# Reordering the second layer of a graph network: attention before the ball mixer, queries kept on chip, two weight jobs in other stages

## The reference, cut to what matters

```
xn = layernorm(x)
x = x + gnn0(xn, W, edges) + mix0(xn)          # message sum; low-rank attention and feed-forward
x = x + ffn0(layernorm(x))                     # 8 experts, all of them
xn = layernorm(x)
x = x + gnn1(xn, src, dst) + mix1(xn)          # the two terms do not depend on each other
x = x + ffn1(layernorm(x))                     # shared expert, and the best 2 of 8 experts

def gnn1(feat, src, dst):
    q, k, v = feat @ Wq.T + bq, feat @ Wk.T + bk, feat @ Wv.T + bv
    score = clip(sum(q[dst] * k[src], per head) / sqrt(32), -10, 10)
    alpha = softmax of score over the edges of one destination
    wv = segment_sum(alpha * v[src], dst)
    x = feat + wv @ Wp.T + bp
    return x + gelu(layernorm(x) @ W1.T + b1) @ W2.T + b2

def mix1(x):                                   # "ball mixer": projections to a ball, a convolution
    ...                                        # (its middle tap only), batch norm, linear attention
```

## Time and profile before

| | us |
|---|---|
| median of 3 runs | 3988.4 |
| lowest, highest | 3985.86, 3989.91 |
| the profiled execution | 3987.43 |
| its span in the profile | 3985.7 |
| granted TensorE clock, mean | 0.807 |

### The profile page before, as it was taken

How to read it: one execution, slowest core, us unless ns; L and a number is a source line. 1 busy time by engine, 2 the same in 40 slices (tenths; PEclk the granted TensorE clock), 3 DMA queues, 4 the chain that set the end, 5 groups by cost and what they waited for, 6 DMA issues and landing times. The chain is left out here.

```text
span 3985.7 us, 66521 instructions
## 1 busy us (share of the span) xinstructions
PE 2587.3 (65%) x17122; PEld 2086.2 (52%) x17123; DVE 2170.5 (54%) x4408; ACT 1269.1 (32%) x2467; POOL 1315.5 (33%) x1017
## 2 busy tenths in 40 slices
PE   4413333436678699996375434777777487699997
PEld 4413333323367477774254423555555366589986
DVE  6523333322456388885237764777777555544445
ACT  0300010003143255553257732222222243345441
POOL 0048888853000000000001024888888500211115
PEclk9855555557679599997597767999999778699998
DMA  1046666730000000001200015777777200356643
GB/s 36 32 105 157 156 165 162 197 94 6 0 22 0 16 11 13 16 16 46 73 0 0 0 40 150 193 189 187 189 191 189 52 21 0 124 188 229 227 159 91
DMA packets 255391, 373.00 MB, mean 94 GB/s; under 512 B 119009, under 2 KB 180889, under 8 KB 250965
## 3 DMA queue, kind: packets, MB, share of 16 engines
q0 software_dynamic: 154752, 174.53, 18.2%
q1 hardware_dynamic: 87700, 185.50, 14.2%
q10 hardware_dynamic: 12864, 12.06, 1.1%
HBM read 320.09 MB, written 50.96 MB: 93 GB/s over the span
## 5 line engine op out<-in xcount | busy, mean ns | idle before, releaser
L750 POOL DMA_INDIRECT ms_got<-gather,ms_index x400 | 506.2, 1265 | 124.9 <-issue 114.4
L1689 POOL DMA_INDIRECT as_gkv<-gather_kv,as_index x340 | 462.0, 1359 | 108.7 <-issue 100.9
L811 PE MATMUL ms_total<-ms_got,ms_hot 125*125 125x256 f16 x1040 | 231.0, 410 | 376.8 <-DMA ms_got<-gather,ms_index 251.9
L811 PEld LDWEIGHTS ms_total<-ms_got,ms_hot 125*125 x1040 | 202.9, 219 | 405.0 <-issue 405.0
L2097 POOL MEMSET bm_fx<- 128x128 f32 x1 | 0.2, 205 | 1013.0 <-POOLq L115 1013.0
L1810 PE MATMUL as_total<-as_gkv,as_hot 125*125 125x264 f32 x850 | 218.8, 406 | 78.0 <-DVE as_summed L555 65.6
L1478 ACT ACTIVATE ex_h<-ex_up,ex_now 128x313 f32<-128x313 f32 (+1 forms) x320 | 196.1, 613 | 197.2 <-PE ex_up L458 190.0
L1810 PEld LDWEIGHTS as_total<-as_gkv,as_hot 125*125 125x125 f32 x850 | 157.7, 193 | 117.8 <-issue 91.8
L2791 DVE CAST moe_hidden<-moe_h 128x256 f16<-128x256 f32 (+1 forms) x336 | 101.8, 303 | 209.9 <-ACT moe_h L2728 209.3
L2728 ACT ACTIVATE moe_h<-moe_up,moe_w 128x256 f32<-128x256 f32 (+1 forms) x336 | 163.1, 487 | 135.2 <-PE moe_up L458 93.2
L1784 PE MATMUL as_picked<-y_rows,as_pick 125*125 x1060 | 150.3, 291 | 52.6 <-issue 47.7
(11 more groups left out here) (448 smaller groups left out, 5895.2 us busy)
## 6 DMA issues: line engine op xcount, KB each, us to landing
moe_w<-wsplit SPq DMA_DIRECT2D x34, 2052.0 KB
as_dsts<-in_dst SPq DMA_DIRECT2D x83, 305.2 KB
wsplit<-ms_split SPq DMA_DIRECT2D x36, 512.0 KB
ms_raw<-in_L_ffn_W1p SPq DMA_DIRECT2D x16, 512.0 KB
ms_raw<-in_L_ffn_W2p SPq DMA_DIRECT2D x16, 512.0 KB
results<-moe_made SPq DMA_DIRECT2D x32, 256.0 KB, 8.2
ms_got<-gather,ms_index POOLq DMA_INDIRECT x400
gather_kv<-qkv_out SPq DMA_DIRECT2D x5, 1250.0 KB
```

The lines of the kernel that those rows point to most:

```text
L750: pool.indirect_dma_start(out=got[:, s, j, :], out_offset=None, in_=m.gather0, in_offset=bass.IndirectOffsetOnAxis(ap=index[:, s, j:j + 1] ...
L811: ins = pe.matmul(total[:, visit % RING, 0:C], hot[:, visit % RING, j, :], got[:, s, j, p * C:(p + 1) * C], start=(j + p == 0), stop=(j + ...
L1689: pool.indirect_dma_start(out=gkv[s][:, j, 0:2 * C], out_offset=None, in_=m.gather_kv, in_offset=bass.IndirectOffsetOnAxis(ap=index[:, s, ...
```

## The change

- The order of the stages: `attention_sum`, `attention_out`, a layernorm and `feed_forward` "ff1" come right behind `query_rows`; `ball_log_rows` and `ball_mixer` come after them, before the last layernorm. `m.y` is taken once and given back before the ball mixer.
- The f16 halves of the queries are written straight into `m.y` (`m.q16`); they are neither stored nor loaded back, and TensorE no longer waits for them in `attention_sum`.
- The turner runs in `edge_tables`: after each of the 20 counting steps TensorE turns one or two blocks, ScalarE copies and stores them before it takes the square root of the degrees.
- The splitter runs in `feed_forward` "ff1" (`splits=True`): 4 steps in each of the first 4 chunks and 2 in the last.
- In `attention_out` the bias bp is a third product per tile (a row of ones with the bias) and no longer an addition on GpSimd.
- `feed_forward` loses its form for several experts, which was not used.

```diff
-def edge_tables(nc, m, src, dst):
+def edge_tables(nc, m, a, src, dst):
...
             @block.scalar
             def _(act):
+                for i in range(2):
+                    turner.load(act, i)
+                turner.store(act)
                 act.wait_ge(s_span, 2)
                 act.activation(m.degree_s[:, 0, :], m.degree_s[:, 0, :], ACT.Sqrt).then_inc(s_rows, 1)
+                turner.finish(act)
...
+                steps, blocks = ET // SET, len(turner.blocks)
+                for i in range(steps):
+                    pe.wait_ge(s_hot, i + 1)
+                    add(i % 2, i == 0, i == steps - 1)
+                    turner.turn(pe, range(blocks * i // steps, blocks * (i + 1) // steps))
...
 def message_sum(nc, m, a):
-        turner = Turner(nc, m, a, ph)
-        splitter = Splitter(nc, m, a, ph)
...
-                        if splits and s % 2:
-                            splitter.low(dve, i, s // 2)
...
-                    turner.turn(pe, part, PARTS)
...
+def feed_forward(nc, m, a, name, W1, b1, W2, gain, bias_in, splits=False):
+    PIECES = 4
...
             def _(sp):
+                sp.dma_start(w1_32, W1.rearrange("(b p) n -> p b n", p=128)).then_inc(s_w, 16)
+                sp.dma_start(w[:, CB * F:].rearrange("p (b n) -> p b n", b=FB),
+                             W2.rearrange("(b p) n -> p b n", p=128)).then_inc(s_w, 16)
+                if splits:
+                    with sp.Fori(0, X8) as e:
+                        for h in range(2):
+                            splitter.move(sp, e, h)
+                    for h in range(2):
+                        splitter.move(sp, X8, h)
+                    splitter.finish(sp)
...
+                def highs(c, own, k):
+                    if splits and (own or k < 2):
+                        for s in range(2):
+                            splitter.high(act, c * PIECES + k, s)
+
+                def chunk(c, own):
+                    for u in range(units):
+                        f, (at, n) = u // 2, HALVES[u % 2]
+                        act.wait_ge(s_up, c * units + (u + 1))
+
+                        act.wait_ge(s_hidden, c * units + max(u - 3, 0) + AHEAD)
+                        act.activation(h32[:, u % 4, 0:n], up[:, u % 4, 0:n], ACT.Gelu,
+                                       scale=1.0 / WS, bias=bias[:, f:f + 1]).then_inc(s_h32, 1)
+                        if u % 8 == 3:
+                            highs(c, own, u // 8)
+                    highs(c, own, 2)
+                    highs(c, own, 3)
...
+                def lows(c, own, k):
+                    if splits and (own or k < 2):
+                        for s in range(2):
+                            splitter.low(dve, c * PIECES + k, s)
...
+                        if u % 8 == 7:
+                            lows(c, own, u // 8)
+                    for j in range(J):
...
+                        if j in (2, 4):
+                            lows(c, own, 1 + j // 2)
...
 def query_rows(nc, m, a):
-                    sp.dma_start(m.gather_q.rearrange("(t p) n -> p t n", p=R)[:, bass.ds(c * J, J), :],
-                                 q16[:, s, :, :, :].rearrange("p j k n -> p j (k n)")).then_inc(s_stored[s], 16)
...
-                        act.activation(q16[:, s, j, 0, :], out[:, s, j, 0:C], ACT.Copy).then_inc(s_high, 1)
+                        act.activation(m.q16[:, c * J + j, 0, :], out[:, s, j, 0:C], ACT.Copy).then_inc(s_high, 1)
...
 def attention_sum(nc, m, dst):
-                sp.dma_start(q16.rearrange("p t k c -> p t (k c)"),
-                             m.gather_q.rearrange("(t p) n -> p t n", p=R)).then_inc(s_q, 16)
...
-                pe.wait_ge(s_q, 16)
...
 def attention_out(nc, m):
-                    for rows_, bias in ((m.z, bp), (m.x, b2)):
-                        some = rows_[:, bass.ds(c * J, J), :]
-                        ins = pool.tensor_tensor(some, some, repeat_mid(bias, J), ALU.add)
-                    ins.then_inc(s_bias, 1)
+                    some = m.x[:, bass.ds(c * J, J), :]
+                    pool.tensor_tensor(some, some, repeat_mid(b2, J), ALU.add).then_inc(s_bias, 1)
...
-                            ins = pe.matmul(bank[:, j % 4, 0:C], cols[:, j, b, :], w[:, b, :],
-                                            start=(b == 0), stop=(b == CB - 1))
+                            pe.matmul(bank[:, j % 4, 0:C], cols[:, j, b, :], w[:, b, :],
+                                      start=(b == 0), stop=False)
+                        ins = pe.matmul(bank[:, j % 4, 0:C], m.ones[0:1, 0:R], bp[0:1, :], start=False, stop=True)
...
         query_rows(nc, m, a)
-        ball_log_rows(nc, m)
-        free_y()
-        ball_mixer(nc, m, a)
-        take_y(1)
         attention_sum(nc, m, a["dst"])
         attention_out(nc, m)
         layernorm(nc, m, "ln5", m.y)
-        feed_forward(nc, m, "ff1", 1, lambda e: m.turned["w1"], col["L1_gnn_b1"], lambda e: m.turned["w2"],
-                     gain=col["L1_gnn_ln_g"], bias_in=col["L1_gnn_ln_b"])
-        free_y()
+        feed_forward(nc, m, a, "ff1", m.turned["w1"], col["L1_gnn_b1"], m.turned["w2"],
+                     col["L1_gnn_ln_g"], col["L1_gnn_ln_b"], splits=True)
+        y_stack.close()
+        ball_log_rows(nc, m)
+        ball_mixer(nc, m, a)
```

More of the change, by code:

```diff
@@ L178, in edge_tables @@
         s_hot, s_count, s_v = ph.sem("hot"), ph.sem("count"), ph.sem("v")
+        turner = Turner(nc, m, a, ph)
         with nc.Block() as block:
@@ L565, in finish @@
         self.dve.sem_inc(s_pace, 1)
[L568 to L608, removed]
-            name, W, o, k, taps = self.blocks[i]
-            kb = k // 128
-            act.wait_ge(self.s_turned, i + 1)
-            if i + 2 < n:
-                self.load(act, i + 2)
-            if i >= 2:
-                act.wait_ge(self.s_out[i % 2], 16 * (i // 2))
-            act.activation(self.cols[:, i % 2, 0:kb, :], self.bank[:, i % 2, 0:kb, :], ACT.Copy)\
-                .then_inc(self.s_cols, 1)
-            act.wait_ge(self.s_cols, i + 1)
-            act.dma_start(self.m.turned[name].rearrange("(b p) n -> p b n", p=128)[:, :, o * 128:(o + 1) * 128],
-                          self.cols[:, i % 2, 0:kb, :]).then_inc(self.s_out[i % 2], 16)
-    def finish(self, act):
-        n = len(self.blocks)
-        act.wait_ge(self.s_out[0], 16 * ((n + 1) // 2))
-        act.wait_ge(self.s_out[1], 16 * (n // 2))
@@ L906, in feed_forward, with part, every_chunk @@
             ph.sem(x) for x in ("up", "h32", "hhigh", "hidden", "down", "added"))
-        ph.ahead(s_h32, s_hidden, s_down, s_added)
+        splitter = Splitter(nc, m, a, ph) if splits else None
+        if splits:
+            splitter.s_pace = s_pace
+        ph.ahead(s_hidden, s_down, s_added, s_h32)
         units = FB * len(HALVES)
         w1_32 = w[:, 0:CB * F].rearrange("p (b n) -> p b n", b=CB)
-        def part(s, k, layer, b, at, n):
+        def part(k, layer, b, at, n):
             start = b * F + at if layer == 0 else CB * F + b * C + at
-            return w16[:, s, k, start:start + n]
+            return w16[:, k, start:start + n]
+        def every_chunk(eng, work):
+            with eng.Fori(0, CHUNKS - 1) as c:
+                work(c, True)
+            work(CHUNKS - 1, False)
         with nc.Block() as block:
@@ L1059, in mixer0 @@
+                every_chunk(dve, chunk)
 def mixer0(nc, m, a):
```

339 lines of the change are left out of this document (135 added, 204 removed).

## The result

The changed kernel takes 4036.9 us (median of 4 runs, 4032.1 to 4045.7) against 3987.1 us (4 runs), a ratio of 1.0128 with a 95% interval of 1.0108 to 1.0149: slower by 1.3%, 6 us under the forecast of 4043 and inside the range. The profiled execution took 4034.7 us, span 4033.0, so it lies 47.3 us over the span before.

What follows compares the result with a forecast made beforehand. GpSimd bounds the message and attention sums, TensorE the second feed-forward, in a chain of stages with barriers. Terms -24 + 15 - 22 - 39 + 7 + 119 = +56 gave 4043 us; 8-in-10 range 3998 to 4090.

Steps and rivals of the forecast that it cites:

- Feed-forward, +119: Second feed-forward: with the split moved in, waits for its loads lengthen the stage by 119 us (ends +55 and +168).
- 17L + 108: Second feed-forward: time from chunk 0's first subtraction to the end, 249 us against 133 before, excluding 3 us for lower clock.
- L: Splitter in the second feed-forward: time from a step's second subtraction until both next halves are loaded, taken as 8.3 us.
- Attention output, +7: Attention output: bias products cost TensorE 2.2 us more a chunk, stage 7 us longer (0 to +10).
- Edge tables, +15: Edge tables: the turner's 26 blocks fit only in part beside the counting steps and delay the square root, +15 us.
- Message sum, -24: Message sum: less stretched gathers save 9 us and the turner's missing tail 14.7 us, together -24 (-19 to -29).
- Queries -22: Queries, keys and values: without the queries' stores, computing becomes the bound, -22 us (-18 to -25).
- attention sum -39: Attention sum: TensorE's first pick no longer waits for queries, so GpSimd never waits for its index, -39 us (-35 to -42).
- (a): Second feed-forward: loads run at nearly full rate, L = 5.2, +3 us, whole kernel 3990 us; chance 0.12.
- (b): Second feed-forward: the split hides almost wholly behind TensorE, L = 4, -17 us, whole kernel 3970 us; chance 0.10.
- (c): Second feed-forward: transfers as slow as in the message sum, L = 10.9, +100 us, whole kernel 4087 us; chance 0.17.
- (d): Attention sum: first pick waits for destinations slowed by gathers, the stage keeps its 39 us, whole kernel 4082 us; chance 0.06.

Runs made afterwards that it cites:

- the nine kernels: Nine kernels, the changed one included, that neither split nor turn weights in the message sum; that stage took 627.6 to 636.0 us, mean 631.5.

## Why the prediction came out right, and its missed term

By its own steps:

- **Feed-forward, +119 against +104.** The mechanism holds, in form and in place. From the first up product to the end it took 2979.7 - 2741.4 = 238.3 us, and 17L + 108 with the measured L of 7.66 is 238.2. That it agrees to 0.1 us is luck: the four rounds of a chunk took 197.4 us where 4 x (4L + 20) is 202.6, and the rest made up for it; with the blocks loaded once the form gives 173.4 us where 179.5 were measured. Off were L, taken as 8.3 (17 x 0.64 = 11 us), a choice between two rows and no measurement, and the 3 us added for the lower clock, which the form didn't need although TensorE was granted only 0.77. (In the kernel before, the first chunk's 96 up products took 15.67 us at a granted 0.82, those of each later chunk 12.97 at 1.00.) The forecast's sign "under 210 us: then L is below 5.5" doesn't fit its own form either, by which 210 us is an L of about 4.8.
- **Attention output, +7 against +25: the failed step.** "Five more cost 2.2 us a chunk" priced a product over one partition by a row of products over 128. Over 65 or 125 partitions that price holds: 46.0 and 47.1 us are +7 and +8. The single partition adds 55.6 - 47.1 = 8.5 us (25 x 0.38 = 9.5 by the rows), and in this execution the clock, which rose 25 us into the stage instead of 6 to 8, another 64.1 - 55.6 = 8.5. The bound of +10 was too low as well: the nearest row had another shape.
- **Edge tables, +15 against +10.4.** The square root is 10.3 us later (118.86, before 108.52). The 4 us of waits that were added for the small blocks did not come: up to the two blocks of eight transposes a counting step begins every 3.26 us. The large ones made TensorE wait for 5.1 us together. One part had no term: ScalarE loads a table for the square root, which it did at 4.24 us before, while it had nothing to do; now it does so behind the last copy, and the square root waits for these 1.28 us.

```profile
117.56 1.28 ACT L315 ACT_TABLE_LOAD   x1 [0.43 <-ACT edg_cols L203]
118.86 0.23 ACT L315 ACTIVATE degree_s<-degree_s 125x25 f32<-125x25 f32 x1
```

- **Message sum, -24 against -27.0**, and against -23.1 for the mean of the nine kernels. The parts were shown apart: the kernel with only the split put back has longer gathers and no tail, the one with only the turner put back has the tail. The tail is 14.6 to 15.0 us each time (15.9 to 16.2 against 1.2 to 1.3); the 9 us for the gathers is a mean over kernels that differ by as much.
- **Queries -22 against -23, attention sum -39 against -38.6.** Both came back when the queries' way through memory did. The 3.5 us of landing and barrier and the 2 us of landing were estimates: before, the next stage began 1.5 us after the last traffic (none from 1940.2 on), and after the change 12.5 us after the last store's issue at 1888.1, where the forecast had 13.6.
- **Rivals.** (a) and (b) needed L of 5.2 and 4. The fixed part of a load behind the 5.2 was an estimate; no run shows one apart. Without stores L was 4.6, with the blocks loaded once 3.85, and there the whole took 3977.5 us, under the kernel before, as the zero at L = 5.0 has it. What stood against them, the megabyte of stores ahead of each load, was the cause. (c) had the gathers' L in a stage without gathers. (d) fell with the first pick 10 us into the stage.

The errors partly cancel: +18 for the attention output, -15, -5, -3, -1 and, in all other stages together, -3.5. With the attention output priced at what it took, the forecast would have been 4061, 24 us too high. So the mechanism of the loss was foreseen, but that the total is only 6 us off is in good part luck.

## What to carry to other kernels

Work that is moved beside a busy engine costs the round trip of its single buffer (7.66 us here), once for every step (17 here), as soon as an engine on the path has to wait for it in order: compute that round trip, with the stores that are issued ahead of the load, and compare it with the slack per step before moving anything. Price a product by a row with the same number of partitions: here one over 1 or 64 between products over 128 cost 0.38 us more than one over 65 or 125, and the row of ones could as well be an identity over all rows. Where a change holds several moves, time each one alone: here the queries on chip gained 58 us and the rest lost 108.

## Not expected of the hardware

- The step between 64 and 65 partitions: 0.38 us a tile for the same two records (1.69 against 1.30 us).
- TensorE's granted clock in a stretch with such products: it rose 6.3 to 43 us into the stage, and differently in kernels that share the stage's code, with TensorE busy for 17.0 to 17.4 of the first 20 us each time.
- 1 MB of stores ahead of 1 MB of loads in the same queue: issued 1.4 us later in the mean of 17 steps, and 1.6 us longer to landing (medians 6.2 against 4.6).
